# First normalisation's result written in phase 1 and loaded in the recurrence, in place of computing it there (Mamba block with a binary MLP, one core)

## The reference, cut to what matters

```python
xn = (x - mean(x)) / sqrt(var(x) + 1e-5)            # x: (8, 512, 128); the first normalisation
x1 = mamba(xn)                                      # _L0_attn_ref, below
out = x + x1 + binary_mlp(xn)

def mamba(xn):
    normed = xn * rsqrt(mean(xn * xn) + EPS) * norm_w
    x_z, z = split(normed @ in_W)                   # 256 channels each
    xc = silu(conv4(x_z) + conv_b)
    dt = clip(softplus(xc @ dt_W + dt_b), 0.001, 0.1)
    Bp, Cp = xc @ B_W, xc @ C_W                     # 64 states
    for t in range(512):                            # h: (8, 256, 64)
        h = exp(dt[t] * A) * h + dt[t] * Bp[t] * xc[t]
        y[t] = sum over n of h * Cp[t]
    x1 = xn + (y * silu(z)) @ out_W
    n2 = rmsnorm(x1, ffn_w)
    return x1 + (silu(n2 @ gate_W) * (n2 @ up_W)) @ down_W
```

## Time and profile before

| | us |
|---|---|
| median of 3 runs | 1106.54 (1098.75 to 1109.56) |
| the profiled execution | 1101.58 |
| its span, first to last instruction | 1099.7 |
| busy TensorE / VectorE / ScalarE / GpSimd | 954.4 / 914.5 / 922.1 / 847.5 |

### The profile page before, as it was taken

One profiled execution on the slowest core, in us unless ns is written; L12 is line 12 of the kernel. 1 busy time (PEld: TensorE's weight loads), 2 busy tenths in 40 slices (PEclk: granted clock), 3 DMA queues, 4 the chain that ended last, 5 costly groups with the idle time before them and its releaser, 6 DMA issues.

```text
span 1099.7 us, 28252 instructions
## 1 busy us (share of the span) xinstructions
PE 954.4 (87%) x8006; PEld 422.2 (38%) x8006; DVE 914.5 (83%) x2035; ACT 922.1 (84%) x1125; POOL 847.5 (77%) x1216
## 2 busy tenths in 40 slices
PE   5988882778999999997998998999989899999898
PEld 3555540113343433332434343334333334343436
DVE  5677672889999999997999997999988799999992
ACT  1656774889999999997999997899998899999981
POOL 6555522789888888897898887898987798989880
PEclk9999996679999999999999999999999899999999
DMA  5245357989999899998799999799999799999940
GB/s 159 102 158 185 142 213 265 388 317 359 353 350 355 297 394 332 374 338 350 290 354 357 356 351 374 254 376 340 356 359 353 258 353 358 358 347 366 385 154 11
DMA packets 81004, 333.74 MB, mean 303 GB/s; under 512 B 15152, under 2 KB 35504, under 8 KB 45488
## 3 DMA queue, kind: packets, MB, share of 16 engines
q1 hardware_dynamic: 80816, 331.60, 81.2%
HBM read 306.38 MB, written 25.17 MB: 301 GB/s over the span
## 4 chain that ended last, share of the span: by engine, by line
PE 22%; DVE 21%; POOL 17%; issue 13%; ACT 2%; DVEq 1%; POOLq 0%; ACTq 0%
POOL decayed L622 15%; DVE ps L1256 8%; PE ps L827 7%; DVE state L1267 7%; PE ps L772 5%; PE ps L926 4%; PE ps L912 3%; DVE h L1364 2%; ACT state L1060 1%; PE ps L890 1%; PE ps L898 1%; DVE gated L1329 1%; POOL base L651 1%; POOL f_nrm L646 1%; POOL f_nrm L634 1%
## 5 line engine op out<-in xcount | busy, mean ns | idle before, releaser
L622 POOL TENSOR_TENSOR decayed<-decay,state 128x256 f32<-128x256 f32 x1024 | 725.3, 734 | 156.1 <-DVE state L1267 111.6
L1040 ACT ACTIVATE decay<-decay,a_col 128x2048 f32<-128x2048 f32 x256 | 514.0, 2008 | 35.2 <-DMA decay<-dt_stage 21.0
L1267 DVE TENSOR_TENSOR state<-decayed,ps 128x256 f32<-128x256 f32 x1024 | 407.1, 417 | 64.3 <-POOL decayed L622 43.1
L1256 DVE TENSOR_TENSOR ps<-decay,ps 128x512 f32<-128x512 f32 x512 | 352.5, 688 | 34.5 <-ACT state L1060 15.8
L827 PE MATMUL ps<-state,c_cols 128*32 128x256 f32 x4096 | 337.2, 402 | 0.0
L1060 ACT COPY state<-ps 128x512 f32<-128x512 f32 x512 | 287.0, 587 | 50.9 <-issue 34.9
L772 PE MATMUL ps<-moving,b_rows 64*128 64x256 bf16 x1024 | 204.2, 280 | 94.3 <-DVE ps L1256 91.3
L779 PE MATMUL ps<-moving,b_rows 64*128 64x256 bf16 x1024 | 205.2, 282 | 15.1 <-DMA b_rows<-b_stage 15.1
L912 PE MATMUL ps<-h,w 128*128 128x256 f32 x512 | 173.0, 423 | 0.8 <-DVE h L1364 0.8
L772 PEld LDWEIGHTS ps<-moving,b_rows 64*128 64x128 bf16 x1024 | 58.1, 94 | 269.6 <-DVE ps L1256 172.1
L827 PEld LDWEIGHTS ps<-state,c_cols 128*32 128x32 f32 x4096 | 82.0, 109 | 113.1 <-issue 105.2
(11 more groups left out here) (124 smaller groups left out, 815.5 us busy)
## 6 DMA issues: line engine op xcount, KB each, us to landing
decay<-dt_stage SPq DMA_DIRECT2D x512, 512.0 KB, 6.4
moving<-u_stage SPq DMA_DIRECT2D x64, 256.0 KB
u_stage<-u_parts SPq DMA_DIRECT2D x16, 512.0 KB, 2.9
b_rows<-b_stage SPq DMA_DIRECT2D x64, 128.0 KB
b_stage<-b_parts SPq DMA_DIRECT2D x16, 384.0 KB, 3.2
dt_stage<-dt_tok SPq DMA_DIRECT2D x8, 512.0 KB, 3.1
moving<-u_stage SPq DMA_DIRECT2D x128, 32.0 KB
x_tok<-in_L_attn_x_dram SPq DMA_DIRECT2D x4, 512.0 KB, 4.0
```

The costliest lines, as they stand in the source:

```text
L622: nc.gpsimd.tensor_tensor(decayed[:, p], decay[:, dec_slot(m, k), p, k % TS, :], state[:, (k - 1) % RING, p * E:(p + 1) * E], ALU.mult).th ...
L1040: nc.scalar.activation(pair, pair, ACT.Exp, scale=a_col[:, 2:3]).then_inc(decay_ready, 1)
L1256: nc.vector.tensor_tensor(ps[:, acc_bank(m, k), :].rearrange("p (q e) -> p q e", q=HQ), decay[:, dec_slot(m, k), HQ:Q, k % TS, :], ps[:, a ...
L1267: nc.vector.tensor_tensor(state[:, k % RING, p * E:(p + 1) * E], decayed[:, p], ps[:, SELFP + k % 2, p * E:(p + 1) * E], ALU.add).then_inc ...
```

## The change

The tokens' first normalisation is computed once more in phase 1: `xn_tokens`, the last stage of VectorE's slot, writes (x - mean) / sqrt(var + eps) of batch s + 1 into a new tile `xnorm` (one buffer), with the mean and nrm[:, 1] that are there. SP stores it to a new HBM tensor `xn_stage` (256 KB a batch), the first two batches ahead of the others' stores, and from then on behind the store of dt. In the recurrence SP loads it into xn, two loads of 64 KB, behind the two of x; TensorE waits for that load in place of the computation, and the six steps k = -7 to 0 go. x itself is still loaded, for `base`, which now waits for it.

```diff
--- before.py
+++ after.py
+    xn_stage = nc.dram_tensor("xn_stage", (B, T, D), F32, kind="Internal").ap()
+        xnorm = c1.enter_context(nc.sbuf_tensor("xnorm", [P, NJ, D], F32))
-        K_STATS, K_MOMENTS, K_RSTD_SUM, K_RSTD, K_SHIFT, K_XN, K_XN_T, K_XN_FEAT = -7, -6, -5, -4, -2, 0, 2, 3
+        K_XN_T, K_XN_FEAT = 2, 3
...
+                def store_xn(n):
+                    wait_all(sp, [(S["xnorm_ready"], n + 1)])
+                    sp.dma_start(xn_stage[n:n + 1].rearrange("o (p j) d -> p o (j d)", j=NJ),
+                                 xnorm[:].rearrange("p j d -> p (j d)").unsqueeze(1)).then_inc(S["xn_stored"], 16)
                 def store(q, bb):
...
                                  ).then_inc(S[f"dt_stored{bb}"], 16)
+                    if n + 2 < B:
+                        store_xn(n + 2)
...
+                store_xn(0)
+                store_xn(1)
                 for q in range(Q):
...
                             sp.wait_ge(S["normed_ready"], n + 2)
+                            sp.wait_ge(S["xnorm_ready"], n + 2)
...
                 sp.wait_ge(S["z_ready"], B)
+                sp.wait_ge(S["xn_stored"], 16 * B)
...
                         sp.dma_start(x_in[:, j, :], x[:, bass.ds(g * TG + j * TC, TC), :]
                                      ).then_inc(G["f_x_loaded"], 16)
+                    for j in range(GT):
+                        sp.dma_start(xn[:, j, :], xn_stage[:, bass.ds(g * TG + j * TC, TC), :]
+                                     ).then_inc(G["f_xn_loaded"], 16)
...
-                    after(pool, "normed_ready", n, back=1)
+                    after(pool, "xnorm_ready", n, back=1)
...
-                    if k == K_RSTD_SUM:
-                        after(pool, "f_mv_ready", g)
-                        after(pool, "f_xn_ready", g, back=1)
-                        nc.gpsimd.tensor_tensor(f_nrm[:, 0], f_mv[:, :, 1], eps_t[:, 0:GT], ALU.add
-                                                ).then_inc(G["f_rstd_sum"], 1)
-                    if k == K_RSTD:
-                        after(pool, "f_rstd_sum", g)
-                        nc.gpsimd.tensor_tensor(f_nrm[:, 1], f_nrm[:, 0], mhalf[:, 0:GT], ALU.pow
-                                                ).then_inc(G["f_rstd_ready"], 1)
...
                     if k == K_BASE:
+                        pool.wait_ge(G["f_x_loaded"], (g + 1) * (16 * GT))
                         after(pool, "f_x1_ready", g)
...
                     if k == K_XN_T:
-                        after(pe, "f_xn_ready", g)
+                        pe.wait_ge(G["f_xn_loaded"], (g + 1) * (16 * GT))
...
-                    if k == K_XN:
-                        after(act, "f_shift_ready", g)
-                        act.wait_ge(G["f_x_loaded"], (g + 1) * (16 * GT))
-                        after(act, "f_x1_ready", g, back=1)
-                        for j in range(GT):
-                            m = nc.scalar.activation(xn[:, j], x_in[:, j], ACT.Identity, bias=f_nrm[:, 4, j:j + 1],
-                                                     scale=f_nrm[:, 1, j:j + 1])
-                        m.then_inc(G["f_xn_ready"], 1)
...
+                def xn_tokens(q, bb):
+                    n = q * 2 + bb
+                    after(dve, "xn_stored", n, per=16, back=1)
+                    for j in range(NJ):
+                        m = nc.vector.tensor_scalar(xnorm[:, j], token_tile(n, j), mean_var[:, bb, j, 0:1],
+                                                    nrm[:, 1, j:j + 1], ALU.subtract, ALU.mult)
+                    m.then_inc(S["xnorm_ready"], 1)
...
                     at(dt_and_u, -1)
+                    at(xn_tokens, 1)
...
-                    if k == K_STATS:
-                        dve.wait_ge(G["f_x_loaded"], (g + 1) * (16 * GT))
-                        after(dve, "f_rstd_ready", g, back=1)
-                        for j in range(GT):
-                            m = nc.vector.bn_stats(f_stats[:, j], x_in[:, j])
-                        m.then_inc(G["f_stats_ready"], 1)
-                    if k == K_MOMENTS:
-                        after(dve, "f_stats_ready", g)
-                        nc.vector.memset(wait_mark[:], 0.0)
-                        for j in range(GT):
-                            m = nc.vector.bn_aggr(f_mv[:, j], f_stats[:, j])
-                        m.then_inc(G["f_mv_ready"], 1)
-                    if k == K_SHIFT:
-                        after(dve, "f_rstd_ready", g)
-                        after(dve, "f_xn_ready", g, back=1)
-                        nc.vector.scalar_tensor_tensor(f_nrm[:, 4], f_mv[:, :, 0], -1.0, f_nrm[:, 1], ALU.mult, ALU.mult
-                                                       ).then_inc(G["f_shift_ready"], 1)
```

More of the change, by code:

```diff
@@ L231, in mamba_and_binary_mlp_block @@
                  "b_copied u_split b_split parts_stored0 parts_stored1 dt_stored0 dt_stored1 pads_ready nrm_step "
-                 "b_zeroed cb_placed u_hi_ready b_hi_ready u_r1_ready b_r1_ready u_mid_ready b_mid_ready w1_step")
+                 "xnorm_ready xn_stored b_zeroed cb_placed u_hi_ready b_hi_ready u_r1_ready b_r1_ready u_mid_ready b_mid_ready w1_step")
         S = {n: sem(n) for n in names.split()}
@@ L286, in mamba_and_binary_mlp_block @@
         y_tok = pb("y_tok", [P, GT, E])
-        f_stats = pb("f_stats", [P, GT, 6])
-        f_mv = pb("f_mv", [P, GT, 2])
-        f_nrm = pb("f_nrm", [P, 5, GT])
+        f_nrm = pb("f_nrm", [P, 2, GT])
         square = pb("square", [P, GT, D])
@@ L638, in finish @@
                         after(pool, "f_n2_ready", g, back=1)
-                        nc.gpsimd.tensor_tensor(f_nrm[:, 2], sumsq[:], inv_d[:, 0:GT], ALU.mult
+                        nc.gpsimd.tensor_tensor(f_nrm[:, 0], sumsq[:], inv_d[:, 0:GT], ALU.mult
                                                 ).then_inc(G["f_mean_square"], 1)
                         after(pool, "f_mean_square", g)
-                        nc.gpsimd.tensor_tensor(f_nrm[:, 2], f_nrm[:, 2], eps_t[:, 0:GT], ALU.add
+                        nc.gpsimd.tensor_tensor(f_nrm[:, 0], f_nrm[:, 0], eps_t[:, 0:GT], ALU.add
                                                 ).then_inc(G["f_rrms_sum"], 1)
@@ L645, in finish @@
                         after(pool, "f_rrms_sum", g)
-                        nc.gpsimd.tensor_tensor(f_nrm[:, 3], f_nrm[:, 2], mhalf[:, 0:GT], ALU.pow
+                        nc.gpsimd.tensor_tensor(f_nrm[:, 1], f_nrm[:, 0], mhalf[:, 0:GT], ALU.pow
                                                 ).then_inc(G["f_rrms_ready"], 1)
                     if k == K_BASE:
+                        pool.wait_ge(G["f_x_loaded"], (g + 1) * (16 * GT))
                         after(pool, "f_x1_ready", g)
@@ L1088, in finish @@
                         for j in range(GT):
-                            m = nc.scalar.activation(n2[:, j], x1[:, j], ACT.Copy, scale=f_nrm[:, 3, j:j + 1])
+                            m = nc.scalar.activation(n2[:, j], x1[:, j], ACT.Copy, scale=f_nrm[:, 1, j:j + 1])
                         m.then_inc(G["f_n2_ready"], 1)
```

4 lines of the change are left out of this document (2 added, 2 removed).

## The result

The changed kernel takes 1106.4 us (median of 20 runs), the kernel before 1102.71 (20 runs beside them): a ratio of 1.0032, interval 1.002 to 1.0045. It is slower by 3.5 us, where a gain of 2.7 was forecast. Both are inside 1%, but the direction is resolved and it is the other one. One of the 20 runs of the changed kernel took 1269.0 us, at a mean granted clock of 0.651 where the others have 0.947 to 0.961, and it is left out of the ratio. The profiled execution took 1107.67 us, its span 1105.8, where the one before took 1101.58: 6.1 us more, so the two profiles lie further apart than the medians.

A forecast was written before the change was run, and what follows sets the result against it. No single engine bounds it: phase 1 follows VectorE's chain, the recurrence a mesh of four engines and DMA. 9.6 + 0.5 - 12.8 = -2.7 us, giving 1103.8 on the scale of the median 1106.54; range 1094 to 1115.

The forecast's parts named there:

- the upper bound for phase 1: Phase 1's added work: 1.1 x 6 + 4.6 + 1.1 = 12.3 us at most, against 9.6 forecast.
- The prediction's own sign of being wrong: Recurrence: the forecast is wrong if ScalarE's waits for decay loads grow well over 4.6 us.
- Slot 0 ... I take 3.0: Phase 1, slot 0: four new VectorE instructions near GpSimd's memset of moving cost 3.0 us, bounds 1.1 and 4.6.
- Slots -1 and 1 to 5, 1.1 us each: Phase 1: the four new VectorE instructions lengthen each of these slots by 1.1 us, 5.5 for slots 1 to 5.
- Slot 6, nothing: Phase 1, last slot: the new 1.1 us lies in VectorE's 1.55 us idle before b_rest, so costs nothing.
- No wait for xn_stored or for SP, DMA free in phase 1: Phase 1: stores have a whole slot (17 us) to land, SP waits anyway, DMA is half free; no cost.
- Removal, 0.8 us a body, 12.8 in all: Recurrence: removed normalisation work gives back 0.8 us a body through TensorE's gaps, 12.8 us for 16 bodies; bounds 4.8 and 18.6.
- the added loads "hidden": Recurrence: two xn loads a body, 0.37 us of DMA, issues hidden in SP's waits; free except in the first body.
- the second rival: Recurrence: chunk and decay loads hold the body, added bytes push landing back; no gain, +11.7 us, 1118; chance 0.14.
- First body +0.5: Recurrence, first body: DMA engines are behind from start to end, so the added loads cost 0.5 us.
- Contention in every slot: Rival, phase 1: new instructions meet GpSimd in every slot, 9 us more in slots 1 to 5; +6.3, 1113; chance 0.07.
- The chain gives all: Rival, recurrence: a body gives back all 1.16 us the chain shows; -8.5 us in sum, 1098; chance 0.19.

The follow-up runs named there:

- Experiment 1: The changed kernel with batch 1's four xnorm instructions moved behind VectorE's own memsets in slot 0: 1098.95 us, 0.9974 of the kernel before.
- experiment 6: The kernel before plus two 64 KB loads a body into a spare tile that nobody reads: 1102.85 us, ratio 1.0016.
- Experiment 5: The kernel before without the normalisation's six steps, x_in read for xn, nothing added in phase 1 and no loads: 1091.14 us, ratio 0.9922.
- kernels 8: The changed kernel with xnorm in VectorE's wait for nrm, and the step 22 decay load issued ahead of the second half chunk: 1089.61 us, 0.99 of before.
- kernel 10: The changed kernel, phase 1 untouched, with the step 22 decay load issued ahead of the second half chunk: 1100.39 us, 0.9999 of the kernel before.
- Experiment 4: The changed kernel with the two xn loads issued after the decay loads of step 26: 1108.64 us, 1.0057 of the kernel before.
- experiment 9: The kernel before with the step 22 decay load issued ahead of the second half chunk: 1100.32 us, ratio 1.0009.
- experiments 2: The changed kernel without the two xn loads a body, x_in read for xn, phase 1 as changed: 1102.18 us, 1.0007 of the kernel before.
- experiment 3: The kernel before plus the phase 1 part alone: xnorm computed and stored, never loaded, normalisation still done in the recurrence: 1126.12 us, ratio 1.0243.

## Why the prediction was wrong, point by point

The time forecast, 1103.8 us, is within 0.3% of the 1106.4 measured and the range holds it, but that is luck: it was counted from the first three runs' median of 1106.54, and 20 runs gave 1102.71. From there the forecast is 1100.0, and it is 6.4 us off. The forecast rested on a balance of two terms of ten microseconds, and both were off to the same side. That the upper bound for phase 1 was 12.3 us, as measured, is luck too: it was made of 4.6 for slot 0 and 1.1 for slot 6, where 7.7 and nothing came. The prediction's own sign of being wrong did show: ScalarE's waits for decay loads grew from 4.6 to 12.7 us.

- **The step that failed first: "Slot 0 ... I take 3.0", with the bound of 4.6.** The slot grew by 7.7. The bound assumed that VectorE can wait for one memset of GpSimd; GpSimd has a second right behind it (L608 before, one row further down than the row I used), and the waiting instruction got in after both. The place was named, the row of the memset was right, and the row behind it wasn't read. Experiment 1 shows that this one item is worth 0.58% between two ratios, 6.4 us. Four such instructions took 1.11 us with GpSimd idle, 4.19 when they were held by one memset, and 7.79 by two. The exclusive lock of the page "SBUF — State Buffer", section "SBUF: two separate sides", in the Trainium skill, held for the whole of one instruction while the other engine is fully blocked, fits the first two; that a blocked instruction can be held through a second one of GpSimd as well, as it was here, the section doesn't state. With both memsets, 1.1 + 2 x 3.5 = 8.1 was the upper end, and the time landed near it.
- **Slots -1 and 1 to 5, 1.1 us each**: right in kind, measured 1.35, 1.0 and four times 0.84 to 0.9. Four instructions of 1.11 us lengthen the slot by a little less. (Slot -1 varies by itself: it is 0.84 us longer in experiment 6 too, which has nothing added there.) The wait for nrm, which was said not to lengthen, went from 1.97 to 2.25 us. **Slot 6, nothing**: right; 1.03 us of the wait of 1.55 was used. With slot 0 this makes 13.5 us, of which 1.2 comes back before the first multiply.
- **No wait for xn_stored or for SP, DMA free in phase 1**: right; no such wait appears, the stores land in 2.2 us (median).
- **Removal, 0.8 us a body, 12.8 in all**: right in the profiled execution, where it stands alone, and too high by the medians. Experiment 5 gives 12.4 us between the multiplies, but 8.6 us by its ratio (6.8 to 10.3); kernels 8 and 10 have recurrences of 882.8 and 880.2 us with everything of the change in them. The reasoning by TensorE's gaps fits the rows. Where the earlier trace rows has four with idle time, there are two after:

```profile
970.43 0.28 PE L779 MATMUL ps<-moving,b_rows 64*128 64x256 bf16 x1 [0.18 <-DVE ps L1264]
975.30 0.28 PE L779 MATMUL ps<-moving,b_rows 64*128 64x256 bf16 x1 [0.86 <-DVE ps L1264]
```

  The first is new, behind VectorE's wait of 0.75 us; the second is the one of 0.74 us before, and the three of 0.41, 0.15 and 0.29 us are gone.
- **The step that failed second: the added loads "hidden".** After, 6.1 us of the 12.8 do not come, where 0.5 was charged. I had priced bytes (0.37 us of a body) and issue time, and had left only 0.14 to the second rival, in which the decay load of the next body comes late and faster engines only arrive sooner and wait. That is the mechanism that was at work, in part: it took half of the gain and not all, so its own price of 1118 us is wrong too. What the forecast had wrong is the cover. It hid the two issues in SP's waits for VectorE, and those waits did shrink (1.9 and 1.5 us in the body shown, against 3.9 and 3.2 in the earlier trace rows), but the decay load for the next body's first step was still issued 0.9 us later in the body than before, and already there it had only 0.1 us between landing and use. That it could be issued sooner, ahead of the half chunk's six issues, is what experiments 8 and 10 use: their recurrences are as short as with no loads. Experiment 4 says that moving the added loads doesn't mend it, experiment 9 that in the kernel before there was nothing to mend, and experiment 5 that the removal alone gives back next to nothing of its gain. The cost needs the loads and the shorter recurrence together.
- **First body +0.5**: not seen; it took 68.11 us against 68.93.
- **Contention in every slot**: excluded, 1.11 us in each of slots 1 to 5. **The chain gives all** (1.16 us a body): not seen; it is 0.8 in experiments 5 and 8 and 0.93 in kernel 10, with its 880.2.

The parts by the ratios are removal -8.6 us (experiment 5) and loads +1.8 (experiment 6), and phase 1, from experiments 2 and 5, which differ in its part alone, 0.85% or +9.4 us. Together +2.6, against 3.5 measured. (With the loads at the 2.8 us between experiment 2 and the change the sum is 3.5 by construction and tests nothing.) The profiled executions show larger pieces (-12.4, +4.8, +12.3, together +4.7) beside the 5.6 us by which the last multiply came later.

## What to carry to other kernels

Work that is moved to where an engine's own list is the chain costs most of its duration (0.84 to 1.0 us a slot of 1.11 here); put into a wait of the same engine, here the one for nrm in the next slot, it cost nothing, and a second buffer of the factors was all that it needed. Before a time is taken for an instruction beside a busy GpSimd, read all of what GpSimd has queued, not the first row of it. And before loads are added to a queue while the engines are made faster, look at which loads land just in time, from landing to use: neither the loads nor the shorter recurrence made ScalarE wait longer for decays here, both together did, and took back half of the gain until the tight load was issued earlier.

## What the runs showed of the hardware that I had not expected

- One VectorE instruction of 0.33 us alone was held through two GpSimd memsets of 3.50 us, back to back: 7.78 or 7.79 us for the four in the changed kernel and in experiments 2, 4 and 10, but 4.19 in experiment 3, which has them as far ahead of the first memset (0.44 us). In the first four the second of the four instructions is held, in experiment 3 only the third, for 3.61 us. What decides that, I can't read off the rows. VectorE's own memset of 3.47 us ran beside GpSimd's without being held: in the kernel before it starts at 19.45, under GpSimd's from 18.73 on, and takes 3.47 us just as it does at 28.44 in the changed kernel, with GpSimd idle.
- A second stall of 2.7 to 3.1 us follows each return of the loop, in experiment 3 alone. VectorE's instructions there are the ones of before; what differs is how much program stands ahead of them. The cause stays open. It is a warning on experiments of this sort: code that is added far away moved the loop by 8 us.
- TensorE's granted clock falls to the lower level (1.2 GHz) at each return of the loop, where TensorE idles for some 5 us: for 6.8 us each in the kernels before and after, for 3.4 to 10.2 in the others. Its mean over the execution was 0.963 before, 0.953 after, 0.956 to 0.962 in the faster kernels and 0.948 in experiment 3. In the loop before and after have the same 0.98; after's lower mean comes from phase 1, which is 0.92 there and 0.97 before. Whether that adds to the 12.3 us no run separates, but slot by slot VectorE's rows account for them.
